# A two-layer network on one core: who rotates when, value sums in pairs, and scores on a quarter of the array

## The reference, cut to what matters

```python
x = L0_attn_x                                   # (4, 2048, 256), float32
xn = layernorm(x)
s = attention0(xn)      # 16 heads of 16; segments of 512 rows, every 8th one a key (64 keys)
                        # scores = q k^T * scale; c = max over each block of 64 query rows, per key
                        # w = exp(scores - c); out = (w v) / (sum(w) + 1e-10); then Wout
g = silu(quantised(xn) @ W^T + bias)            # quantised: rounded to fp8 and back
x = x + s * g
xn = layernorm(x)
s = attention1(xn)      # rotary positions on q and k, causal, 16 heads of 16
g = silu(mixture_of_8_experts(xn))              # top 2, limited places
x = x + s * g
```

## Time and profile before

| | |
|---|---|
| median of 3 runs | 3812.4 us (3809.0 to 3821.1) |
| the profiled execution | 3820.8 us, its span 3819.0 us |
| first stage | up to about 964 us |
| busy over the span | PE 3249.5, DVE 2754.2, ACT 2004.4, POOL 651.7 us |
| mean granted TensorE clock | 0.924 of full speed |

### The profile page before, as it was taken

The page is one execution under the profiler, slowest core; times in us unless marked ns, Lnnn a source line. Parts: engine busy times, 40 slices in busy tenths (PEclk is TensorE's granted clock), DMA queues, the critical chain, the costliest instruction groups (busy, mean ns, idle before and its releaser), DMA issues. The chain is left out here.

```text
span 3819.0 us, 67859 instructions
## 1 busy us (share of the span) xinstructions
PE 3249.5 (85%) x22678; PEld 1773.4 (46%) x22679; DVE 2754.2 (72%) x5118; ACT 2004.4 (52%) x3363; POOL 651.7 (17%) x954
## 2 busy tenths in 40 slices
PE   5878878877398898899899899999979899999977
PEld 2434434434133333333333333333348788888865
DVE  5777777776778888788788888888725565555547
ACT  2333333333057777788788788788852232222224
POOL 1132222222122232000000000000023323223310
PEclk9999999998579999999999999999989999999989
DMA  2122222222422211222222112220031121111149
GB/s 72 50 71 67 61 67 67 61 67 67 86 43 46 45 19 32 47 46 45 47 46 45 21 31 46 46 46 18 17 108 63 39 78 44 59 54 45 45 131 332
DMA packets 252770, 230.55 MB, mean 60 GB/s; under 512 B 60924, under 2 KB 235132, under 8 KB 252156
## 3 DMA queue, kind: packets, MB, share of 16 engines
q1 hardware_dynamic: 236040, 192.39, 19.9%
q0 software_dynamic: 16384, 33.64, 2.8%
HBM read 124.28 MB, written 101.06 MB: 59 GB/s over the span
## 5 line engine op out<-in xcount | busy, mean ns | idle before, releaser
L1474 ACT ACTIVATE at_ex<-at_so,keep_exp_scale 128x512 f32<-128x512 f32 (+1 forms) x2304 | 1350.6, 673 | 447.9 <-PE at_so L1368 241.4
L1501 DVE TENSOR_REDUCE at_best<-at_p 128x1 f32<-128x512 f32 (+3 forms) x2560 | 1393.3, 603 | 261.4 <-PE at_p L1350 162.9
L1350 PE MATMUL at_p<-at_ks,at_qs 48*128 48x512 f16 (+3 forms) x2560 | 811.4, 370 | 165.6 <-DVE at_best L1501 123.7
L1368 PE MATMUL at_so<-at_qs,at_ks 50*128 50x512 f16 (+3 forms) x2560 | 694.5, 362 | 18.7 <-issue 9.5
L1422 PE MATMUL at_ob<-at_ex,at_vs 128*32 128x512 f32 (+3 forms) x5120 | 608.3, 567 | 0.5 <-issue 0.4
L1772 ACT ACTIVATE e_hh<-e_hb,e_b1now 128x512 fp32r<-128x512 f32 x256 | 174.5, 690 | 595.5 <-PE e_hb L1707 541.6
L1657 POOL DMA_INDIRECT e_xg<-s_xn,e_token x128 | 143.4, 1121 | 1695.7 <-DVE e_token L1802 1523.8
L1350 PEld LDWEIGHTS at_p<-at_ks,at_qs 48*128 48x128 f16 x2560 | 216.9, 94 | 459.3 <-DVE at_best L1501 393.1
L1368 PEld LDWEIGHTS at_so<-at_qs,at_ks 50*128 50x128 f16 x2560 | 200.1, 95 | 464.6 <-ACT at_ex L1474 346.4
L1737 PE MATMUL e_ob<-e_w2h,e_hh 128*128 128x256 f32 x1024 | 298.5, 292 | 15.7 <-DVE e_og L1840 15.1
L1738 PE MATMUL e_ob<-e_w2l,e_hh 128*128 128x256 f32 x1024 | 294.4, 288 | 0.0
(11 more groups left out here) (209 smaller groups left out, 4651.6 us busy)
## 6 DMA issues: line engine op xcount, KB each, us to landing
s_v<-a_v SPq DMA_DIRECT2D x64, 256.0 KB, 3.2
s_qk<-a_part SPq DMA_DIRECT2D x128, 128.0 KB, 2.4
at_vs<-s_v SPq DMA_DIRECT2D x32, 512.0 KB
s_eo<-at_empty SPq DMA_DIRECT2D x16, 1024.0 KB
e_w<-w SPq DMA_DIRECT2D x16, 1024.0 KB
f_rows<-s_eo SPq DMA_DIRECT2D x32, 512.0 KB, 8.4
at_qs<-s_qk SPq DMA_DIRECT2D x96, 128.0 KB
at_ks<-s_qk SPq DMA_DIRECT2D x96, 128.0 KB
```

What stands on the lines that cost most here:

```text
L1350: last = pe.matmul(out, qs[rows, buf, p, qt * P:(qt + 1) * P], ks[rows, buf, p, ch * SEG:ch * SEG + w], start=True, stop=ch != qc)
L1368: last = pe.matmul(so[:, v % NST, at:at + w], ks[rows, r, p, kt * P:(kt + 1) * P], qs[rows, r, p, q0:q0 + w], start=True, stop=not diag)
L1474: ev.done(act.activation(ex[:, v % NE, 0:width], so[:, v % NST, 0:width], ACT.Exp, scale=keep["exp_scale"][:, 0:1]), "ex")
L1501: ev.done(dve.tensor_reduce(best[:, row:row + 1, ch], p1[:, (at + e) % NP1, 0:wide(item)], AX, ALU.max), "mx")
```

## The change

- GpSimd's `rotate(n)` waits for VectorE's finished half (`rot`), no longer for the projections.
- `wexp` has four buffers in place of two. The scores go through four banks, two of `sc` and the two of `tb`, so that a score may run up to three ahead of the block maxima. They use only the 32 rows of `kbd` and `qT` that carry the pair.
- The sums are issued two at a time, behind scores 3, 5 and 7, and at the end; each of the first of two waits for both exponentials. The turns come one pair of scores later.
- Since `tb` now holds scores, `turn_second(n)` and `second_turned(n)` move behind the last sums. `part0(n - 1)` moves from behind exponential 3 to behind exponential 6.
- On VectorE `normalise(m, 2)`, `normed_tokens(m + 1, 0)` and `rest(n - 1)` move behind the pairs; the first step of `residual` is split off and stands ahead of `rest`.

```diff
@@ -148,6 +148,7 @@
         bqk1 = sb("bqk1", [P, 4])
         wvg1 = sb("wvg1", [P, DC, D + E])
         bv1 = sb("bv1", [P, D])
+        NW = 4
         x = sb("x", [P, 2, TT, D])
         stats = sb("stats", [P, 2, TT, 6])
         mv = sb("mv", [P, 2, TT, 2])
@@ -168,7 +169,7 @@
         vbd = sb("vbd", [P, H // 2, 2 * HW])
         keymax = sb("keymax", [P, 2, NBLK])
         shifted = sb("shifted", [P, 2, SEG])
-        wexp = sb("wexp", [P, 2, SEG])
+        wexp = sb("wexp", [P, NW, SEG])
         oT = sb("oT", [P, 2, SEG])
         den = sb("den", [P, TT, G])
         rden = sb("rden", [P, TT, G])
@@ -203,6 +204,10 @@
         sc = ps("sc", [P, 2, SEG])
         ob = ps("ob", [P, SEG])
 
+
+        def bank(p):
+            return sc[:, p % 4, :] if p % 4 < 2 else tb[:, p % 4 - 2, :]
+
         NP0 = H // 2
         counts = dict(
             var=1, rstd=1, xn=1, tr=1, trc=2, q=2, qc=2, kv=1, kvc=1, ff=2, ffc=2, quant=1, clip=1, round=2, wide=3,
@@ -324,7 +329,7 @@
 
                     st.step(n)
                     cos, sin = rotary(n % SPB)
-                    ev.wait(pool, "pjc", n, 4)
+                    ev.wait(pool, "rot", n, 1)
                     ev.wait(pool, "p2", n, 0)
                     st.then(pool.tensor_tensor(rot[:, :, 1, :], qk[:, :, 0, :], sin, ALU.mult))
                     st.then(pool.tensor_tensor(prod1[:], qk[:, :, 1, :], cos, ALU.mult))
@@ -428,19 +433,20 @@
                     f, a = p // (NP0 // DC), 2 * (p % (NP0 // DC))
                     if a == 0:
                         ev.wait(pe, "qc", m, f + 1)
-                    ev.wait(pe, "shift", m, max(p - 1, 0))
-                    ev.done(pe.matmul(sc[:, p % 2, :], kbd[:, f, a:a + 2, :].rearrange("p a k -> p (a k)"),
-                                      qT[:, f, :], start=True, stop=True), "s")
+                    ev.wait(pe, "shift", m, max(p - 3, 0))
+                    rows = slice(a * HD, (a + 2) * HD)
+                    ev.done(pe.matmul(bank(p), kbd[rows, f, a:a + 2, :].rearrange("p a k -> p (a k)"),
+                                      qT[rows, f, :], start=True, stop=True), "s")
 
                 def values(m, p):
-                    ev.wait(pe, "wexp", m, p + 1)
+                    ev.wait(pe, "wexp", m, p + 2 - p % 2)
                     if p == 0 and m >= 2:
                         ev.wait(pe, "vjc", m - 2, TT)
                         ev.wait(pe, "lc", m - 2, TT)
                     if p % 2 == 0:
                         ev.wait(pe, "oc", m, p // 2)
                     r = (p % 2) * 2 * HW
-                    ev.done(pe.matmul(ob[r:r + 2 * HW, :], vbd[:, p, :], wexp[:, p % 2, :], start=True, stop=True), "pv")
+                    ev.done(pe.matmul(ob[r:r + 2 * HW, :], vbd[:, p, :], wexp[:, p % NW, :], start=True, stop=True), "pv")
 
                 def turn(m, g):
 
@@ -526,13 +532,16 @@
                     n, more = m - 1, m + 1 < NSEG
                     for p in range(NP0):
                         scores(m, p)
-                        if n >= 0 and p == 2:
-                            turn_second(n)
-                        if p >= 1:
-                            values(m, p - 1)
                         if p >= 3 and p % 2 == 1:
-                            turn(m, (p - 3) // 2)
+                            values(m, p - 3)
+                            values(m, p - 2)
+                        if p >= 5 and p % 2 == 1:
+                            turn(m, (p - 5) // 2)
+                    values(m, NP0 - 2)
                     values(m, NP0 - 1)
+                    turn(m, 2)
+                    if n >= 0:
+                        turn_second(n)
                     gate(m, 0)
                     turn(m, 3)
                     gate(m, 1)
@@ -655,15 +664,15 @@
                     n, more = m - 1, m + 1 < NSEG
                     for p in range(NP0):
                         ev.wait(act, "shift", m, p + 1)
-                        ev.wait(act, "pv", m, max(p - 1, 0))
-                        ev.done(act.activation(wexp[:, p % 2, :], shifted[:, p % 2, :], ACT.Exp, scale=SCALE), "wexp")
-                        if p == 2 and n >= 0:
-                            second_turned(n)
-                        if p == 3 and n >= 1:
+                        ev.wait(act, "pv", m, max(p - NW + 1, 0))
+                        ev.done(act.activation(wexp[:, p % NW, :], shifted[:, p % 2, :], ACT.Exp, scale=SCALE), "wexp")
+                        if p == 6 and n >= 1:
                             part0(n - 1)
-                        if p >= 2 and p % 2 == 0:
-                            out_copy(m, p // 2 - 1)
+                        if p >= 3 and p % 2 == 1:
+                            out_copy(m, (p - 3) // 2)
                     out_copy(m, 3)
+                    if n >= 0:
+                        second_turned(n)
                     half_tanh(m, 0)
                     half_tanh(m, 1)
                     projected(n, 0)
@@ -805,7 +814,7 @@
 
                     ev.wait(dve, "s", m, p + 1)
                     ev.wait(dve, "wexp", m, max(p - 1, 0))
-                    blocks = sc[:, p % 2, :].rearrange("p (n q) -> p n q", q=BLK)
+                    blocks = bank(p).rearrange("p (n q) -> p n q", q=BLK)
                     st.then(dve.tensor_reduce(keymax[:, p % 2, :], blocks, AX, ALU.max))
                     st.settle()
                     st.mark(dve.tensor_tensor(
@@ -837,12 +846,14 @@
                         scalar=in_scale[:, 0:1], in1=fbias[:].unsqueeze(1).to_broadcast([P, 2, D]),
                         op0=ALU.mult, op1=ALU.add), "ffc", m)
 
-                def residual(st, m):
-
-                    ev.wait(dve, "ez", m, 2)
-                    st.mark(dve.scalar_tensor_tensor(out=z[:], in0=ez[:], scalar=1.0, in1=z[:],
-                                                     op0=ALU.add, op1=ALU.mult), "gate", m)
-                    st.settle()
+                def residual(st, m, half):
+
+                    if half == 0:
+                        ev.wait(dve, "ez", m, 2)
+                        st.mark(dve.scalar_tensor_tensor(out=z[:], in0=ez[:], scalar=1.0, in1=z[:],
+                                                         op0=ALU.add, op1=ALU.mult), "gate", m)
+                        return
+                    ev.wait(dve, "gate", m, 1)
                     for f in range(2):
                         ev.wait(dve, "so", m, f + 1)
                         st.mark(dve.scalar_tensor_tensor(
@@ -916,18 +927,20 @@
                             second_norm(st, n, 1)
                         if p == 1:
                             quantise_rest(st, m)
-                        if p == 4 and n >= 1:
-                            rest(st, n - 1)
-                        if p >= 3 and p % 2 == 1:
-                            normalise(st, m, (p - 3) // 2)
-                        if p == 5 and more:
-                            normed_tokens(st, m + 1, 0)
+                        if p >= 5 and p % 2 == 1:
+                            normalise(st, m, (p - 5) // 2)
+                    normalise(st, m, 2)
                     gated(st, m, 0)
                     normalise(st, m, 3)
                     gated(st, m, 1)
                     if more:
+                        normed_tokens(st, m + 1, 0)
+                    residual(st, m, 0)
+                    if n >= 1:
+                        rest(st, n - 1)
+                    if more:
                         normed_tokens(st, m + 1, 1)
-                    residual(st, m)
+                    residual(st, m, 1)
                     second_norm(st, m, 0)
                     values1(st, n, 0)
                     if more:
```

## The result

The changed kernel takes 3873.8 us in the median of four runs, the kernel before 3814.7 in its four: ratio 1.0153, interval 1.0128 to 1.0178. It is slower, by 59 us, and outside the range. The profiled execution took 3867.1 us, its span 3865.2, and it was the fastest of the four.

A forecast was written before the change was run, and what follows sets the result against it. Neither engine was taken as the bound throughout: VectorE paces the score part, TensorE the dense part. Middle segments +5, first two -10 and tail +10 gave +5 on 3812.4, about 3818 us; range 3765 to 3862.

The forecast's parts named there:

- (a): Rotation: with GpSimd behind VectorE's half, VectorE's three instructions shrink to 3×1.22, first block maximum 3.85 us earlier per segment.
- (b): Start of the score part: GpSimd's rotation holds VectorE's four normalisations (`L768`) behind the first pair; price 5.4 us.
- rival 1: Score part: the normalisations are not held by GpSimd, score part 2.8 us shorter, total about 3773 us; chance 0.16.
- (e): Score part on TensorE: pairs of sums and the 32-row scores overlap; it saves little.
- rival 4: Score part: 32-row scores, or the pairs, don't overlap, about 1 us twice, +28, total 3846 us; chance 0.06.
- (g): Dense part: GpSimd's twelve statistics steps held beside gate product and `rest`, TensorE stalls 3.2 us, lower clock +0.5.
- rival 3: Dense part: GpSimd's twelve statistics steps slip between VectorE's work, no stall, total about 3762 us; chance 0.08.
- (f): Score part: TensorE's low clock ends at 19 us, gate 27.3 us behind the first maximum; net clock term +0.6 us.
- rival 2: Score part: TensorE's low clock lasts to the gate, gate at about 30 us, total 3857 us; chance 0.18.
- the +0.5 behind the stall: Dense part: the gap while TensorE waits for the normalised tokens may lower its clock, +0.5 us per middle segment.
- (h): First two segments: score part falls by some 6 to 7 us, dense stall costs 1 to 3; together -10 us.
- (i): Tail: GpSimd's last rotation starts later, +7.05 us, held normalisations one segment earlier, +2.6; together +9.7 us.

The follow-up runs named there:

- the mended one: Changed kernel with scores on 128 rows, GpSimd's rotation behind the next segment's predicated copy, and statistics ahead of the last normalises: 3688.3 us; again on 32 rows 3741.8 us.
- two other mends: Changed kernel with GpSimd's rotation behind the predicated copy, 3799.1 us, and changed kernel with statistics ahead of the last normalises, 3784.2 us.
- The four mends: Changed kernel with one edit each: GpSimd's rotation waiting as before 3828.4 us, 128-row scores 3812.7, GpSimd behind the predicated copy 3799.1, statistics ahead of the last normalises 3784.2.
- the first wait filled: Changed kernel with scores 0 to 3 issued three times each on all 128 rows, so TensorE works through its first wait: 3887.6 us.
- GpSimd as before: Changed kernel with GpSimd's rotation waiting for the projections, as in the kernel before: 3828.4 us.
- the rotation order alone: Kernel before with one edit, GpSimd's rotation waiting for VectorE's half: 3842.3 us.
- GpSimd behind the copy: Changed kernel with GpSimd's rotation waiting until VectorE has passed the next segment's predicated copy: 3799.1 us; the same edit on the kernel before: 3798.1 us.
- the statistics earlier: Changed kernel with the next segment's statistics back ahead of the last normalises: 3784.2 us.
- the later f16 copy: The mended one with ScalarE's f16 copy behind the last copy of sums in place of between exponentials 6 and 7: 3644.4 us.

## Why the prediction was wrong

*Steps that held.* (a) VectorE's three rotation instructions took 1.22, 1.22 and 1.23 us, 3.84 less than in rows 3, forecast 3.85. (b) The normalisations are held as the walk had it: 6.41 us for the four, 5.0 more, forecast 5.4. The doubt about `L768` is settled, and rival 1 is out; the Trainium skill's rule (SBUF — State Buffer, Who interferes with whom) agrees, with these 6.41 us beside it. (e) Both kinds of pairs overlap, rival 4 is out. (g) The twelve steps took 6.1 us and the stall is 3.09 against 3.2 forecast; rival 3 is out, and removing it brought at least its price.

*The step that failed* is (f), the clock term. I took the gate at 27.3 us behind the first maximum, with the low level ending at 19 us. It came at 29.5, and the low level lasted to the gate and beyond: this is rival 2, whose 29.8 was given 0.18. But rival 2's time, 3857, was too low as well, since it ended the low level at the gate. So the terms that were mis-sized are the net clock term of the score part (the gate's delay at 1.3 us, measured 3.5) and the +0.5 behind the stall. Two losses in the dense part were missing or too small: the gate's own first half at low clock (2.28 in place of 1.49), and the products behind the stall (1.63 and 3.08 in place of 1.04 and 1.88), 1.8 us against 0.5. Worked out for a middle segment, with the one of rows 2 and 3 (56.05) as the base: -3.84 for the rotation, +3.5 for the score part (29.5 less 26.0), +3.1 stall, +0.8 gate, +1.8 behind the stall: 61.4, which is what is measured. Against the mean periods, 61.1 less 56.7 over fourteen segments is 62 us.

What caused it, as far as the runs show: the size of (f) rested on how long TensorE would be busy, and I had counted a score on a quarter of the rows as work like any other. With scores on 128 rows and nothing else changed, the clock was up by the second sums in every middle segment. In the six kernels with 32-row scores whose first sums ran at the low level it was never up by the second sums, not even where TensorE was kept as busy. That one line is worth 61 us in the changed kernel and 53 in the mended one. The part of the change that was costed at next to nothing, since it saved little, was among the dear ones.

It is not the whole cause. Keeping TensorE busy on 32 rows gave back 30 of the 61 us, and two other mends that left the scores on 32 rows had the clock up 9.5 us behind the first sums. Why the low level lasted 19.7 us in the changed kernel and about 9 us in those two, over the same work, stays open.

The rule of the Trainium skill that I cited (TensorE: Matmul & The Clock Gate, PE-mode transpose), that turns don't count as busy, pointed to the same rival; no run here changes the turns alone, so it stays untested.

*Smaller terms.* The sum of 3812.4 and 5 is 3817, not 3818. (h) the first two segments were to bring 10 us; the third segment's predicated copy comes 5.2 earlier (148.3 against 153.5 us), half of that. (i) the tail, from the last segment's predicated copy to ScalarE's last f16 copy, grew by 8.5 us, from 73.7 to 82.2; forecast 9.7. The stage ends 60.3 us later by that copy (1024.8 against 964.6), which agrees with the loss of 59 between the medians. The two profiled executions as wholes differ by only 46 us, since the untouched stages behind took 2840 us in one and 2854 in the other.

*Where the single losses overlap.* The four mends, each alone, give 45, 61, 75 and 90 us, and the whole loss is 59: each also shortens the time at the low clock, so their gains overlap. A single gain is not the price of what was mended, either. Kernels with different edits settle on the same period: the changed one and the one with the first wait filled on 61.4 us, GpSimd as before and the rotation order alone on 58.0, GpSimd behind the copy and the statistics earlier on 54.6. That the clock has a part in this is likely, since it changes its level at the same place in nearly every settled segment there; how was not tested. What the change brought besides, and the losses hid, is the shorter score part: with the three mends and the later f16 copy the gate is at 18.8 us in place of 26.0.

Open: what the pairs of sums and the four banks are worth each, apart from the moved work, was not run.

## What to carry to other kernels

Where a wait is lifted between two engines that share a resource, look at what the late one meets next: the hold of 3.85 us became one of 5.0 us on the path. Don't read "32 rows, overlapping" as a saving while TensorE is waiting for others anyway; look at the granted clock behind the next wait first, and keep full-row products if they fit into the idle time. Don't add the gains of single mends, and where only one stage was changed, compare its own end in the traces as well as the total. And before moving statistics to where the engine is free, count the chain of small steps on the other engine that must end before their result is used, with all that this engine is held by on the way.

## What the runs showed of the hardware

- A stretch of sums, turns and scores on 32 of 128 rows left TensorE's granted clock at 0.50 for 15.8 us, 15.4 of them busy; the same with scores on 128 rows was at 1.00 after 5.6 us, 5.5 of them busy. In two other kernels sums and turns with scores on 32 rows were back at the upper level within 9.5 us.
- A wait of 2.95 us behind 32-row scores was followed by the lower level although TensorE had worked without a pause for 26 us shortly ahead of it (492.2 to 517.9). In the kernel before, a wait of 2.94 us behind full-row scores was followed by sums at the upper level (1.04).
- Four records of 64-column sums took as long as two, at either level (1.98 against 1.97, 1.08 against 1.04 to 1.07 us), and the eight records of four 32-row scores 1.1 us together.
- GpSimd steps on 4 columns, 0.20 us alone, took 1.11 beside a VectorE product of 1.22 and 2.12 beside one of 2.28; VectorE tensor_scalar instructions with two scalars per partition took up to 2.5 us in place of 0.41 beside GpSimd products.
